# Three-hop graph kernel on one core: dense units moved out of the table and list stages into the second hop and around the third

## The reference

```
feats, cur = [x], x                       # x: 100000 x 256, float32
for _ in range(3):
    cur = segment_sum(weight[:, None] * cur[src], dst, 100000)   # 25000 edges
    feats.append(cur)
y = x + concat(feats, 1) @ shared_weight + bias                  # shared_weight: 1024 x 256
out = layernorm(y)                        # per row, no scale or shift
```

## Time and profile before

| | |
|---|---|
| runs | 1682.57 us (median), 1680.76 to 1683.73, 3 runs |
| profiled execution | 1681.41 us, of it the span from first to last instruction 1679.5 us |
| busy in the span | PE 1567.3, PEld 1335.7, DVE 1169.2, ACT 1145.9, POOL 1065.6 us |
| granted PE clock, mean | 0.978 of 2.4 GHz |
| DMA | 451.09 MB, mean 269 GB/s |

### The profile page before, as it was taken

How to read it: one execution, slowest core, us unless ns; L and a number is a source line. 1 busy time by engine, 2 the same in 40 slices (tenths; PEclk the granted TensorE clock), 3 DMA queues, 4 the chain that set the end, 5 groups by cost and what they waited for, 6 DMA issues and landing times.

```text
span 1679.5 us, 36209 instructions
## 1 busy us (share of the span) xinstructions
PE 1567.3 (93%) x8468; PEld 1335.7 (80%) x8468; DVE 1169.2 (70%) x4883; ACT 1145.9 (68%) x3038; POOL 1065.6 (63%) x1044
## 2 busy tenths in 40 slices
PE   6799999999999999978978999969999999999993
PEld 5688888888888888757757888758888888888882
DVE  6867777777777778986644545437777777777773
ACT  3687777777777766656754655537777777777774
POOL 2277777777777731556774555547777777777764
PEclk9999999999999999999989999989999999999996
DMA  7499999999999986658986777767888888888852
GB/s 254 164 354 337 338 335 338 338 335 336 329 332 338 341 273 232 215 173 276 365 277 180 210 211 202 182 184 260 274 265 276 278 278 280 283 275 271 269 197 91
DMA packets 217722, 451.09 MB, mean 269 GB/s; under 512 B 30444, under 2 KB 125993, under 8 KB 217622
## 3 DMA queue, kind: packets, MB, share of 16 engines
q1 hardware_dynamic: 167730, 343.20, 58.5%
q0 software_dynamic: 49456, 106.58, 22.3%
q10 hardware_dynamic: 436, 0.20, 0.0%
HBM read 232.78 MB, written 225.74 MB: 273 GB/s over the span
## 4 chain that ended last, share of the span: by engine, by line
PE 77%; DVE 10%; issue 5%; DMA 3%; POOL 2%; ACT 1%; DVEq 0%; POOLq 0%; SPq 0%; ACTq 0%
PE ps_y L1218 32%; PE ps_u L1284 9%; PE ps_xT L1209 8%; PE ps_sum L1251 6%; PE ps_sum L1423 5%; PE ps_u L1423 5%; PE ps_u L1278 3%; DVE y_ring L1492 3%; PE ps_list L1384 2%; PE ps_u L1384 2%; DVE stats L1498 2%; PE ps_u L1417 1%; PE ps_sum L1417 1%; DMA c_rows<-sums,scatter_idx 1%; PE ps_u L1377 1%
## 5 line engine op out<-in xcount | busy, mean ns | idle before, releaser
L1218 PE MATMUL ps_y<-w_sb,xT 128*128 128x256 f32 x3128 | 808.5, 385 | 16.0 <-DVE y_ring L1492 16.0
L1218 PEld LDWEIGHTS ps_y<-w_sb,xT 128*128 128x128 f32 x3128 | 566.3, 193 | 78.2 <-issue 16.3
L1492 DVE TENSOR_TENSOR y_ring<-ps_y,bias 128x512 f32<-128x512 f32 x391 | 270.0, 691 | 251.4 <-PE ps_y L1218 250.5
L943 ACT ACTIVATE o_ring<-y_ring,shift,rstd 128x256 f32<-128x256 f32 (+1 forms) x782 | 421.7, 590 | 0.1
L930 ACT COPY xT<-ps_xT 128x512 f32<-128x512 f32 x391 | 227.3, 581 | 202.3 <-PE ps_xT L1209 194.5
L1498 DVE BATCH_NORM_STATS2 stats<-y_ring 128x6 f32<-128x256 f32 (+1 forms) x782 | 291.3, 415 | 4.8
L707 POOL DMA_INDIRECT tails_found<-tail_keys,table_idx x200 | 201.0, 1005 | 124.0 <-issue 69.9
L1209 PE MATMUL ps_xT<-ident,x_ring 128*128 128x128 f32 x1564 | 240.6, 277 | 23.7 <-ACT xT L930 14.7
L707 POOL DMA_INDIRECT rows_in<-in_x,gather_idx x200 | 202.4, 1012 | 81.7 <-issue 68.7
L711 POOL DMA_INDIRECT out_rows<-u_out,tailo_idx x197 | 197.4, 1002 | 85.8 <-issue 39.9
L707 POOL DMA_INDIRECT rows_in<-in_x,tailx_idx x197 | 201.8, 1024 | 77.7 <-issue 47.0
(11 more groups left out here) (231 smaller groups left out, 2100.2 us busy)
## 6 DMA issues: line engine op xcount, KB each, us to landing
x_ring<-in_x SPq DMA_DIRECT2D x195, 512.0 KB, 5.9
out_rows<-o_ring SPq DMA_DIRECT2D x195, 512.0 KB, 4.0
c_rows<-zeros SPq DMA_DIRECT2D x50, 512.0 KB
c_rows<-sums SPq DMA_DIRECT2D x50, 512.0 KB
u_rows<-u_out SPq DMA_DIRECT2D x50, 512.0 KB, 4.0
keys_bc<-keys_out SPq DMA_DIRECT2D x64, 256.0 KB, 5.1
keys_bc<-u_rows SPq DMA_DIRECT2D x25, 512.0 KB, 5.5
tails_found<-u_rows SPq DMA_DIRECT2D x12, 512.0 KB
```

The lines of the kernel that those rows point to most:

```text
L943: last = act.activation(o_ring[slot][0:rows, r * D:(r + 1) * D], y_ring[k][0:rows, r * D:(r + 1) * D], ACT.Identity, bias=shift[k][0:rows, ...
L1218: last = pe.matmul(ps_y[bank][0:rows, r * D:(r + 1) * D], xT[bank][:, q * P:q * P + rows], w_sb[:, c, :], start=c == 0, stop=c == KC - 1)
L1492: dve.tensor_tensor(y_ring[k][0:rows, half * 2 * D:(half + 1) * 2 * D], ps_y[half][0:rows, :], bias2[0:rows, :], ALU.add).then_inc(y_copie ...
```

## The change

Tables have 3, 2 and 1 units in their steps, not 3, 3, 3; list steps have 2 units, not 3; B steps 4, not 3; the bridge before the third hop is a step of 3 and one of 2, not one of 2; after the third hop's loop comes a new step of 4. The total stays 195. A keeps 50, C 20 and D 72 units. ACT and DVE get tables for steps of 4 and of 1.

The part of the table work that makes the bf16 parts (L1625 to L1642) moves into the eight slots of A's first step (`fix_parts`), and PE waits for `tables_ready` at A's third step. The late-tile search moves into B: its node part into B's second step (`find_late`), its count into B's third. DVE handles the first two pairs before it waits for the edge loads, and SP loads the bias before the edges. Of the 50 zero blocks, 12 are now written in the last two table steps (6 each), one in each of A's 25 steps, and 13 in list steps 1 to 7.

```diff
-    TABLE_STEPS = 3
-    A_UNIT = STEP * TABLE_STEPS
+    TABLE_UNITS = (STEP, PAIR, 1)
+    A_UNIT = sum(TABLE_UNITS)
-    B_UNIT = LIST_UNIT + STEP * LIST_ALL
+    B_UNIT = LIST_UNIT + PAIR * LIST_ALL
-    BRIDGE_UNIT = B_UNIT + STEP * B_STEPS
+    BRIDGE_UNIT = B_UNIT + FOUR * B_STEPS
-    C_UNIT = BRIDGE_UNIT + PAIR
-    D_UNIT = C_UNIT + PAIR * FIRST_GROUPS
+    C_UNIT = BRIDGE_UNIT + STEP + PAIR
+    D_UNIT = C_UNIT + PAIR * FIRST_GROUPS + FOUR
...
-        bridge_step = (BRIDGE_UNIT, PAIR, 0, STEP)
+        bridge_b = ((BRIDGE_UNIT, STEP, 0, FOUR), (BRIDGE_UNIT + STEP, PAIR, 0, STEP))
+        bridge_c = ((D_UNIT - FOUR, FOUR, 0, PAIR),)
...
             # SP
             sp.dma_start(w_sb[:, :, :], ...)
+            for k in range(2):
+                sp.dma_start(bias2[:, k * D:(k + 1) * D], bias.partition_broadcast(P)).then_inc(bias_loaded, 16)
...
+            sp.wait_ge(blank, 6)
             for s in range(1, TABLE_STEPS):
                 store_and_load(table_step(s))
-            sp.wait_ge(blank, 6)
+                for k in range(TABLE_FILLS // 2):
+                    zero_c2(A_FILLS + (s - 1) * (TABLE_FILLS // 2) + k)
...
-                zero_c2(2 * a)
                 store_c1(a, 0)
                 load_ahead(dense, 1)
-                zero_c2(2 * a + 1)
+                zero_c2(a)
...
                 store_and_load(list_step(l))
+                for k in range(2):
+                    if zeroed < ZERO_FILLS:
+                        zero_c2(zeroed)
...
             C_TILE = TILES + G * n_groups
-            store_and_load(bridge_step)
+            for dense in bridge_b:
+                store_and_load(dense)
...
                 group_c(g)
+            for dense in bridge_c:
+                store_and_load(dense)
...
             # PE
             def step_a(a, dense, place):
+                if isinstance(a, int) and a == 2:
+                    pe.wait_ge(tables_ready, 1)
...
-            pe.wait_ge(tables_ready, 1)
...
                     sum_tile(TILES + Q * b + q, q % 2, q % G, q)
+                    if b == 2 and q == 3:
+                        pe.wait_ge(late_ready, 1)
+                        pe.matmul(ps_list[0:1, 0:LATE0], ones[:, 0:1], late_f[:, 0:LATE0], start=True, stop=True).then_inc(late_spread, 1)
...
             # DVE
-            PAIR_AT = {STEP: {1: 0, 2: 1, 3: 2, 5: 3, 6: 4, 7: 5}, PAIR: {1: 0, 3: 1, 5: 2, 7: 3}}
+            PAIR_AT = {FOUR: {q: q for q in range(Q)}, STEP: {1: 0, 2: 1, 3: 2, 5: 3, 6: 4, 7: 5},
+                       PAIR: {1: 0, 3: 1, 5: 2, 7: 3}, 1: {3: 0, 7: 1}}
...
+            dve.wait_ge(bias_loaded, 32)
+            for q in range(4):
+                dense_slot(table_step(0), q)
             dve.wait_ge(edges_loaded, 16 * 17)
...
                     dense_measure(dense, q)
+                    if isinstance(a, int) and a == 0:
+                        fix_parts(q)
...
                     dense_slot(b_step(b), q)
+                    if b == 1:
+                        find_late(q)
+                    if b == 2 and q == 5:
+                        dve.wait_ge(late_spread, 1)
...
-            for q in range(Q):
-                dense_slot(bridge_step, q)
+            for dense in bridge_b:
+                for q in range(Q):
+                    dense_slot(dense, q)
             for q in range(G):
                 dve.wait_ge(gathered[q], C_GATHERS)
...
                 copy_v(G * n_groups - G + k, k, n_groups - 1)
+            for dense in bridge_c:
+                for q in range(Q):
+                    dense_slot(dense, q)
```

171 lines of the change are left out of this document (90 added, 81 removed).

## The result

Twelve runs of each kernel: before 1683.4 us in the median (1680.69 to 1685.49), after **1677.59 us** (1674.43 to 1679.87), a ratio of 0.9967 with a 95% interval of 0.996 to 0.9975. The change makes the kernel 5.8 us faster. The forecast was 1671: the direction held and the time lies in the stated range, but less than half of the forecast 11.9 us came. In the ratios of the experiments, an execution far longer than its fellows is left out (one of 3861.94 us, of the last run with both edits).

A forecast was written before the change was run, and what follows sets the result against it. PE was taken to bound the kernel wherever it does not wait. Terms -18.9 + 3.0 - 27.6 + 12.7 + 8.3 + 10.6 = -11.9 us gave 1671 us, range 1657 to 1687 for 8 times in 10.

The forecast's parts named there:

- Where the latency is 8.4, a step is 8.4 + 3.9 = 12.3: List steps 3 to 7: DVE newly waits for entries, bounds 11.6 and 12.9 us; four steps give -10.6.
- Steps over 13 us: List: steps over 13 us were named as a sign that the forecast is wrong.
- steps 0 to 2: List: step 0 from 14.9 to 11.7 us, step 1 from 13.7 to 9.5, step 2 from 15.6 to 11.3.
- the last step and the chain over SP: List's end: last step -1.5 us; entries to B's first tile, through SP's key store, -3.8 us.
- Tables, -16.2 for -18.9: Tables: fewer units and moved work save DVE 21.9 us; A's first tile 18.9 us sooner, bounds -14 and -22.
- What is left is bound by DVE's chain still: Tables after the change: DVE's chain still binds the stage and PE waits for it.
- Start of A, +0.6 for +3: A's start: zero blocks ahead of key loads and u stores make these late, +3 us, bounds 0 and +9.
- The rule of the Trainium skill: A's start: engines go round between queue rows, so POOL's gathers pass the zeros; +3 us stays, without it near 9.
- Second hop, +12.1 for +12.7: Second hop: 20 units for 15, DMA tight with 36.3 MB; 107.5 us, +12.7, bounds +9 and +24.
- Rival 3: Second hop: DMA binds B's five steps at 304 GB/s, 119 us; total +18, 1689 us; chance 0.20.
- Bridges, +9.7 for +8.3 and +13.1 for +10.6: Ahead of C +8.3 us, ahead of D +10.6, PE waiting about 5 us at each; D's landing about 4.
- Rival 2: Bridges hide nothing: waits of 7.6 and 11.2 us return whole; 9.4 us more, 1680 to 1683 us; chance 0.15.

The follow-up runs named there:

- the last run with both edits: Changed kernel with C's first indices written between the two bridge steps and zero blocks back in the first hop, fourth run: 1948.84 us of 1974.68, ratio 0.9884.
- the quiet list: Changed kernel, zero blocks in the first hop, unit loads and stores in list steps 1 to 8 cut to one 1 KB row: list stage 130.4 and 130.8 us.
- The square: Table stage with nine or six units, table work kept in or moved out: nine 58.3 and 58.2 us, six 49.8 and 42.2 us.
- the first run between the bridges: Changed kernel with C's first indices written after the bridge's first three units, D's ahead of its bridge: 1925.95 us of 1954.19, ratio 0.9858 to the kernel before.
- the run with the gathers first: Changed kernel with first gather indices of C and the tail, and SP's keys and loads, ahead of the bridge units: 1669.19 us, 0.9912 of the kernel before.

## Why the prediction was wrong

**The failed step is the list's: "Where the latency is 8.4, a step is 8.4 + 3.9 = 12.3".** The mechanism was there as written (a wait of DVE for entries in the steps, staging to landing plus 4 us), but the term was mis-sized: the latency is 9.8 us, the step 13.8. Four steps gained 4.5 us (59.6 to 55.1) where 10.6 stood in the sum. That is 6.1 of the 9.7 us by which the profiles miss the forecast. I had read the latency off steps in which no zero block was issued, and had the 13 blocks that the change puts there in mind only for the first hop. They cost 3.4 of the 6.1 between these two profiles. The other 2.7 us lie with the units' own loads and stores: without these the wait for entries went, and the four steps took 2.1 to 3.1 us less (49.0 against 51.1 to 52.1). The forecast read 7.1 and 8.9 us off the last groups of the list; the four steps as forecast are 49.0 us (59.6 less 10.6), which is what the quiet list took. Steps over 13 us stood in the forecast as a sign of being wrong. The rest of the list's sum was right: steps 0 to 2 gained 12.4 us (forecast 11.7), the last step and the chain over SP 5.4 (5.3).

**Tables, -16.2 for -18.9.** The bounds (-14 and -22) held. The forecast added DVE's savings as if the stage stayed DVE's: "What is left is bound by DVE's chain still". The square says otherwise: units are worth 8.5 and the work 7.6, not 10.3 and 11.6 less 3, and with nine units the work is worth nothing. The terms were too large as well: DVE's busy time fell by 18.1 us (50.35 to 32.23), not 21.9. In the changed kernel DVE is busy 32.2 of 42.2 us. What holds each of the other 10 is open; ScalarE's block of counts is excluded.

**Start of A, +0.6 for +3.** The zero blocks ahead of the keys delayed nothing that PE had to wait for. The forecast let 2 MB of them go before A starts and the rest at 350 GB/s; measured are 417 GB/s from 45 to 61 us. The rule of the Trainium skill that I cited (DMA: Bandwidth & Descriptors, section on queues, rings and completion order), by which gathers pass the pile, is borne out in part at most: the first gather's packets began 4.9 us after its issue behind the pile and 2.0 without it, and in the list gathers land 0.9 us later beside two blocks. Why they were held is not shown. That it cost nothing is due to the lead of four tiles that the gathers have, and in so far the small cost was luck and not the reasoning of the forecast.

**Second hop, +12.1 for +12.7.** Right, and closer to PE's bound than taken: PE busy 105.2 of 106.9 us. DMA moved 348 GB/s, above the 328 that gave the 111 us of the forecast. Rival 3 did not come near its 24 us a step (21.4). The loop after it is 1.0 us shorter, which was not in the sum. The 358 GB/s of the Trainium skill (section on bandwidth of the same page) were not passed in this stage's mean, but they are no cap: 417 GB/s were moved from 45 to 61 us, most of it writes of zeros.

**Bridges, +9.7 for +8.3 and +13.1 for +10.6.** Waits of 5.4 and 7.8 us, both behind what DVE stages after its slots: the mechanism of the forecast, shown by moving the staging (with the keys and loads of SP, at D not told apart). The wait of the kernel before was in part another: there the indices were written in time, and POOL's first gather left 1.3 us after the last scatter had landed. The forecast took both for the same. The second is too small by the landing, 6.9 us from issue (1102.39) to D's tile (1109.30) where I took about 4 "with the loads mostly done": SP issues the four loads of u at 1099.27 to 1101.05, behind its own bridge slots, so they are as much in the way as before. C and D are 1.0 us longer each, forecast 0.

**Sum.** +2.7 - 2.4 + 5.4 - 0.6 - 1.0 + 1.4 + 1.0 + 2.5 + 1.0 = +10.0, for the 9.7 us between forecast and profiled span (the rest is rounding and an earlier start); the medians keep 6.6 of them (1671 to 1677.6), since the profiled execution after lies above its median. Rival 2's time (1680 to 1683) came nearest in the profiles, but not by its way: the bridges were 3.9 us dearer than forecast where it had 9.4, and the list fell short.

**Where the gain went.** The list gave 22 us, and second hop and tail took all of it back (1677.36 against 1677.59 with the list undone). The tables gave 16.2 for 9.7 in the bridge, 6.5 net, near the measured 5.8 us. But the 9.7 is counted from the bridge of the kernel before (21.5). With the second hop as changed, a bridge of two units takes 18.3, and beside that the three moved units cost 14 us for the 16 that they save. Writing the first gathers' indices, and asking for their keys and loads, ahead of the units that were to cover them is worth more than the whole change: 1669.19 us, the fastest kernel on that chip, with the stage ahead of C still 3.5 us over the changed kernel's; with C's indices written between the two bridge steps the stage is about 4 us shorter than with the indices last, shown on the other chips alone.

## What to carry to other kernels

Work put in as cover hides a wait only if what is waited for is set going before it, on every engine whose program it passes: here the index writes of one engine, the loads of another. And where it must itself wait (an index buffer still in use), it belongs in the middle of the cover, not at its head.

A latency read off a stage holds for the transfers of that stage: when the change also adds transfers there, they lengthen the latency and not only the sum of bytes.

Two engines near each other's load are worth little alone: taking 10 us from the fuller gained 0.1, taking units too gained 16. Price such edits as the larger of the engines after each, not as a sum of savings. And price a moved unit against the stage as it will be after the other edits, not as it was.

## What the runs showed of the hardware

The same kernels took 16 to 17% longer on three other chips (before: 1954.19, 1954.57, 1969.98 and 1974.68 us). It lies in three stages, first hop, second hop and D (without its end): 677, 124 and 631 us in the first run between the bridges, where the changed kernel has 541, 107 and 531. C's 40 tiles without the loop, with the least traffic (193 GB/s), took 189.3 us there and 189.1 in the run with the gathers first. Windows of the first hop of that run, against the second row of the first fence above:

```profile
53.01:735.50 682.49, 575.08 (x3031) 466.75 (x3032) 402.74 (x1814) 421.36 (x1334) 395.55 (x392) 0.97 0.77 252
```

252 GB/s at a DMA share of 0.77, for 313 at 0.94, and PE idle for 107 us of it. The waits of ScalarE in it, by releaser (us, times, longest), of which the kernels on the first chip have none that ends with "remote", that is, with something that the profile does not show:

```profile
ACT xT L956 <- remote: 73.2, 19, 5.5
...
ACT rows_in L1015 <- remote: 40.1, 30, 3.0
```

These are pauses of up to 5.5 us. The quiet list has them too, of 2.5 us, at 3 to 6 GB/s, so at least those are not contention with the kernel's own transfers. What they are is not shown. The tables took the same there and here; the list without zero blocks 132.4 to 134.7 us, for 130.2.

PE's clock fell to its lower level, 1.2 GHz, after a wait of 4.87 us: eight matmuls took 3.75 us for 1.89 (at 853.59 above). The clock is not what set the list's steps: the third and fourth were granted 1.00 in the changed kernel and 0.87 and 0.86 in the mean without the zero blocks, and were 0.9 and 1.05 us shorter all the same.
